# Binary convolution and gated state-space block on one core: order of small steps between two long stages

## The chip, the cores and the metric

The kernel runs on one core of a Trainium2 chip. The time is that of one execution on the device in microseconds, the median of the runs shown. The profile is taken by the hardware profiler from one execution.

## The reference, cut to what matters

The input x is 16 x 112 x 112 x 256, float32. Layer 0 is a group norm, the sign of it, a depthwise 3x3 convolution with signed weights and a residual. Layer 1 takes a group norm of that and

```python
ca_gate = sigmoid(fc(avg) + fc(mx))            # per image and channel
xc = x * ca_gate
m = mean(xc, channels)                          # one value a pixel
y = _s6(m, A, d_w, d_b, B_w, B_b, C_w, C_b)     # scan over the 12544 pixels, 16 states
s = conv7x7([mean(xc), max(xc)], lsa_w)         # per pixel
x2 = xc * sigmoid(y) + xc * sigmoid(s)
out = (x2 - mean(x2)) * rsqrt(var(x2) + EPS) * bn_gamma + bn_beta   # over batch and pixels
return x + relu(out)
```

The scan is h = a * h + b per state, with a = exp(delta * A), and y = sum(h * c). The mean and variance of x2 run over all images, so every x2 is needed once for the statistics and again for the output.

## The kernel before, in words

There are three blocks (`nc.Block`), each with one program an engine. The first makes layer 0 and the channel gates image by image and stores its result x1 in DRAM (`x1_scratch`). It ends with the scans of the first group of 8 images.

The second block is the one the change touches. It has two stages.

*Scans of the second group.* The pixels of the 8 images come in 14 chunks of 896, numbered n = 14 to 27 (NCG = 14, NC = 28). SP loads for each chunk two sets of rows (`load_rows`, L539) and a broadcast row set of 448 KB (`load_spread`, L548) into rings of four places. ACT turns the latter into decays (`make_decay`, L612), PE makes the input of the scan with `spread` (four matmuls, L631), DVE scans (`scan`, L604), PE sums the states with `read_out` (eight matmuls, L640), ACT evacuates y (`evac_y`, L619), and SP stores it to `y_scratch` (L556). In PE's loop the order is: spread of chunk n + 1, at most one *product* (two matmuls, L648), read-out of chunk n. A product is one of 14 steps of the 7x7 convolution over a half of the second group's images. 14 of the first half and 10 of the second stand ahead of the first spread, the other four in chunks 14 to 17. SP's order in chunk n is: load_rows and load_spread of chunk n + 4, store of y of chunk n - 1.

y comes back from DRAM in another layout (`load_y`, L438), in two parts: rows 0 to 63 and rows 64 to 111 of the images, each in two halves q = 0 and q = 1. SP loads q = 0 and POOL q = 1. `load_y` waits until the chunks that it needs are stored. On part 0, DVE joins y (`join_y`, L1746 and L1747) behind scan 25, ACT makes the sigmoids (L1702, L1686), and DVE splits the gate into three bf16 parts (`split_gate`, L1755 to L1760) behind scan 27.

The gates of the last image, which is resident, are stored to `gate_scratch` row by row (`store_last`, L415: four stores for each of three split parts q) and loaded back as 12 rows a strip (`load_gate`, L1562). In part 0 SP, ACT and POOL store one q each, in part 1 SP stores two and POOL one. `store_gates` (L424, 12 stores on POOL) does the same for the other images.

*Statistics.* An image has 7 strips (NS = 7), and xt has one place a strip (`slots`). For each of 112 strips PE broadcasts the gate (L1574, four matmuls), DVE makes u in two operations (L1787, one for each half of the channels), ACT squares it (L1717). SP loads the next image's strip into the place as soon as DVE is done with it (`load_slot`, L1568, 1792 KB, and its gate). In the first strip's turn DVE joins part 1, and in the second's it splits part 1. SP starts with place 0 when all gates of the last image are loaded. After the last strip DVE reduces the sums and makes scale and shift (L1808 to L1833), and makes the first strip of the next pass (`first_strip`, L1799, one for each half j).

The third block, the last pass, makes u again (L2008), applies relu on ACT (L1979), adds x1 on DVE (L2026), transposes on PE (L1958), evacuates on ACT (L1991) and stores (L1928), while SP loads the strips again (L1916).

Of the kernel before, what the change touches and what calls it, by code (L numbers as in the profile page):

```python
# [5 lines left out]
def binary_conv_then_gated_ssm_block(  # L6
# [30 lines left out]
    ACT = mybir.ActivationFunctionType  # L37
# [46 lines left out]
    with ctx:  # L84
# [1526 lines left out]
        bn_ln = sem("bn_ln")  # L1611
        bn_exp = sem("bn_exp")
        gate_ps3 = [banks(psum[:, b * 2048:(b + 1) * 2048], BW) for b in range(2)]

        U3, Q3 = 3, 4

        with nc.Block() as block:
            @block.sync
            def _(sp):
# [14 lines left out]
                for n in range(NCG, NC):  # L1634
                    if n + NROW1 < NC:
                        load_rows(sp, n + NROW1)
                    if n + ND1 < NC:
                        load_spread(sp, n + ND1)
                    if n > NCG:
                        store_y(sp, n - 1)  # L1640
                    if n == NCG + NA:
                        load_y(sp, 1, 0, 0)
                store_y(sp, NC - 1)
                load_y(sp, 1, 0, 1)
                for part in range(2):
                    sp.wait_ge(split_made, 2 + part)
                    store_last(sp, part, 0)
                    if part:
                        store_last(sp, part, 1)
                    sp.wait_ge(last_out[0], 32 * BR * (part + 1))  # L1650
                    sp.wait_ge(last_out[1], 16 * BR * (part + 1))
                    for s in strips_of(part):
                        sp.sem_inc(arrived3[s], 16)
                        load_gate(sp, arrived3, 0, s)
                sp.wait_ge(gates_out, 48 * BR)

                def step(it, more):
                    for n in range(NN):
                        if n < NS or more:
                            sp.wait_ge(u_made3, it * (2 * NN) + 2 * (n + 1) + U3)  # L1660
                            load_slot(sp, arrived3, it * 2 + n // NS, it * 2 + n // NS + 1, n % NS)

                step(0, True)
                sp.wait_ge(gates_out, 96 * BR)
# [5 lines left out]
            @block.gpsimd  # L1670
            def _(pool):
                load_y(pool, 0, 1)
                load_y(pool, 1, 1, 0)
                store_gates(pool, 0, 0, GI)
                pool.wait_ge(split_made, 2)
                store_last(pool, 0, 2)
                load_y(pool, 1, 1, 1)
                pool.wait_ge(split_made, 3)
                store_last(pool, 1, 2)
                store_gates(pool, 1, 0, GI - 1)  # L1680

            @block.scalar
            def _(act):
# [10 lines left out]
                for n in range(NCG, NC):  # L1694
                    if n + 2 < NC:
                        make_decay(act, n + 2)
                    if n > NCG:
                        evac_y(act, n - 1)
                    if n == NC - 3:
                        act.wait_ge(s_made, 4)  # L1700
                        for b in range(2):
                            ins = nc.scalar.activation(s_out[1][:, b * IB * W:(b + 1) * IB * W], s_ps[b], ACT.Sigmoid)  # L1702
                        ins.then_inc(s_sig, 1)
                        sigmoid_y(1, *part_rows(0))
                evac_y(act, NC - 1)
# [6 lines left out]
                def squares3(it):  # L1712
                    for n in range(NN):
                        for j in range(NJ):
                            act.wait_ge(u_made3, it * (2 * NN) + 2 * n + j + 1 + U3)
                            u = xc[n % 2][:, j, :]
                            nc.scalar.activation(u, u, ACT.Square,  # L1717
                                                 accum_out=g2_p[:, n, j, bass.ds(it, 1)]).then_inc(squared3, 1)
# [6 lines left out]
                act.wait_ge(bn_ln, 1)  # L1725
                nc.scalar.activation(bn[:, 5, :], bn[:, 4, :], ACT.Exp, scale=-0.5).then_inc(bn_exp, 1)

            @block.vector
            def _(dve):
# [34 lines left out]
                for n in range(NCG, NC):  # L1764
                    scan(dve, n)
                    if n == NC - 3:
                        join_y(1, 1, *part_rows(0))
                    if n == NC - 1:
                        split_gate(1, 1, *part_rows(0))
# [67 lines left out]
            def _(pe):  # L1837
# [8 lines left out]
                pe.wait_ge(conv_late, 32)  # L1846
                spatial_products(1, 0, 10)
                spread(pe, NCG)
                for n in range(NCG, NC):
                    if n + 1 < NC:  # L1850
                        spread(pe, n + 1)
                    k = 10 + n - NCG
                    spatial_products(1, min(k, 2 * KS), min(k + 1, 2 * KS))
# [19 lines left out]
        u_made4 = sem("u_made4")  # L1873
        relu_made = sem("relu_made")
        x2_made = sem("x2_made")
# [28 lines left out]
        with nc.Block() as block:  # L1904
# [62 lines left out]
            def _(act):  # L1967
# [4 lines left out]

                def relu(it, m):

                    h = m // NS % 2
                    for j in range(NJ):
                        act.wait_ge(u_made4, count(it, m, NJ) + j + 1)
# [3 lines left out]

                relu(0, 0)

# [83 lines left out]
```

## Time and profile before

| | us |
|---|---|
| median of 3 runs | 3281.78 (3280.92 to 3282.52) |
| the profiled execution | 3279.52 |
| its span in the profile | 3277.8 |
| DVE busy | 2972.6 |
| ACT busy | 2703.5 |
| PE busy | 2541.6 |
| POOL busy | 53.2 |

The span is what the profile shows from the first to the last instruction; the profiled execution took 1.7 us more. Busy times are sums over the span. The granted clock of TensorE was 0.849 of full speed on average. All times of rows are from the start of the span.

### The profile page before, as it was taken

The numbers are of one execution on the slowest core, as the hardware profiler recorded it, in microseconds if no ns is written. First come the engines' busy times: TensorE is split into PE (matmuls) and PEld (weight loads), VectorE is DVE, ScalarE is ACT, GpSimd is POOL, SyncE is SP. The second block draws the span as 40 slices with busy tenths as digits, with TensorE's granted clock in tenths as the row PEclk, the third lists the DMA queues.
The fourth block names the chain that finished last, engine by engine and source line by source line (L and its number), as shares of the span: only waits on it lengthen the run. The fifth ranks groups of instructions, "written<-read, shape, count | busy, mean of one in ns | idle before, by whom it ended". The sixth has DMA issues, their size and how long they took to land. (4 is left out here: it accounts for less than half of the span.)

```text
span 3277.8 us, 50171 instructions
## 1 busy us (share of the span) xinstructions
PE 2541.6 (78%) x17105; PEld 1636.8 (50%) x17105; DVE 2972.6 (91%) x4057; ACT 2703.5 (82%) x3772; POOL 53.2 (2%) x103
## 2 busy tenths in 40 slices
PE   7899999999999999999988333333567667666766
PEld 5566666666666666666542000000456555555555
DVE  8789999899998999899987999999999999999997
ACT  6788888888888888888774788888799888888887
POOL 3000000000000000000001100000000000000000
PEclk9999999999999999999997555555688877778777
DMA  8899999999999999999866699999699999999998
GB/s 312 322 373 408 375 369 372 371 406 378 371 371 370 408 377 374 370 373 394 280 187 169 273 421 422 420 420 417 241 429 428 429 429 429 429 429 429 429 429 361
DMA packets 199099, 1228.50 MB, mean 375 GB/s; under 512 B 29793, under 2 KB 38937, under 8 KB 157645
## 3 DMA queue, kind: packets, MB, share of 16 engines
q1 hardware_dynamic: 196012, 1223.42, 92.6%
q0 software_dynamic: 2720, 1.97, 0.3%
q8 instruction: 139, 2.28, 0.3%
q14 instruction: 100, 0.81, 0.1%
q10 hardware_dynamic: 128, 0.01, 0.0%
HBM read 805.14 MB, written 420.17 MB: 374 GB/s over the span
## 5 line engine op out<-in xcount | busy, mean ns | idle before, releaser
L1455 PE MATMUL psum<-signs,taps 128*128 128x448 f16 x4032 | 858.9, 356 | 39.4 <-DVE signs L1084 30.3
L1574 PE MATMUL psum<-signs,picked 12*128 12x448 bf16 x896 | 315.7, 493 | 339.3 <-DMA signs<-gate_scratch 278.9
L1455 PEld LDWEIGHTS psum<-signs,taps 128*128 128x128 f16 x4032 | 385.7, 98 | 367.2 <-DVE signs L1084 49.0
L2008 DVE SCALAR_TENSOR_TENSOR xc<-xt,curs,psum 128x1792 f32<-128x1792 f32 x222 | 452.1, 2078 | 56.4 <-PE psum L1574 44.0
L847 ACT ACTIVATE xt<-psum 128x896 f32<-128x896 f32 x416 | 378.3, 911 | 141.6 <-PE psum L1353 126.0
L1787 DVE SCALAR_TENSOR_TENSOR xc<-xt,curs,psum 128x1792 f32<-128x1792 f32 x224 | 455.9, 2078 | 32.1 <-PE psum L1574 30.6
L1717 ACT ACTIVATE xc<-xc 128x1792 f32<-128x1792 f32 x224 | 380.1, 1697 | 94.1 <-DVE xc L1787 94.0
L1135 DVE CUSTOM_DVE_ANT_0 xt<-work,xt 128x896 f32<-128x896 int8 x416 | 436.0, 1085 | 14.3 <-ACT work L855 14.3
L1353 PE MATMUL psum<-ident,stage 128*128 128x128 f32 x3066 | 409.6, 276 | 20.9 <-POOL over_c L805 6.4
L1979 ACT ACTIVATE xc<-xc,bn,curs 128x1792 f32<-128x1792 f32 x224 | 411.7, 1903 | 13.3 <-issue 4.5
L863 ACT ACTIVATE work<-xt,mean 128x1792 bf16<-128x1792 f32 x208 | 370.3, 1780 | 35.6 <-DVE x1max_p L1135 35.6
L1353 PEld LDWEIGHTS psum<-ident,stage 128*128 128x128 f32 x3066 | 353.5, 142 | 68.6 <-issue 22.0
L1958 PE MATMUL psum<-ident,last_unit 128*128 128x128 f32 x1568 | 277.8, 350 | 140.7 <-DVE last_unit L2026 66.9
L1958 PE MATMUL psum<-ident,signs 128*128 128x128 f32 x1568 | 269.4, 341 | 133.6 <-DVE signs L2026 57.7
L1991 ACT ACTIVATE stage<-psum 128x512 f32<-128x512 f32 x525 | 275.3, 611 | 95.1 <-DMA out_dram<-stage 68.0
L1574 PEld LDWEIGHTS psum<-signs,picked 12*128 12x128 bf16 x896 | 84.4, 114 | 535.3 <-DVE xc L1787 378.1
L1958 PEld LDWEIGHTS psum<-ident,last_unit 128*128 128x128 f32 x1568 | 253.0, 213 | 179.7 <-ACT stage L1991 66.5
L1958 PEld LDWEIGHTS psum<-ident,signs 128*128 128x128 f32 x1568 | 244.1, 211 | 171.4 <-ACT stage L1991 70.5
L1222 DVE TENSOR_TENSOR stage<-xc 128x896 f32<-128x896 f32 x224 | 243.8, 1088 | 61.2 <-ACT xc L894 54.1
L1232 DVE TENSOR_REDUCE pmax<-psum 128x4 f32<-128x512 f32 x448 | 257.6, 617 | 38.7 <-PE psum L1402 36.0
L1084 DVE SCALAR_TENSOR_TENSOR signs<-xt,mean,signs 128x896 f16<-128x896 f32 x208 | 240.3, 1155 | 7.4
L855 ACT ACTIVATE work<-psum,border 128x896 int32<-128x896 f32 x224 | 224.2, 1001 | 18.7 <-PE psum L1455 18.6
(221 smaller groups left out, 2951.9 us busy)
## 6 DMA issues: line engine op xcount, KB each, us to landing
xt<-x_scratch SPq DMA_DIRECT2D x210, 1792.0 KB, 25.3
stage<-x_dram SPq DMA_DIRECT2D x219, 896.0 KB, 9.9
xc<-x_scratch SPq DMA_DIRECT2D x210, 896.0 KB, 9.3
x_scratch<-xt SPq DMA_DIRECT2D x208, 896.0 KB, 9.2
out_dram<-stage SPq DMA_DIRECT2D x75, 1792.0 KB, 21.9
out_dram<-work SPq DMA_DIRECT2D x37, 1792.0 KB, 21.9
x_scratch<-last_unit SPq DMA_DIRECT2D x16, 896.0 KB, 9.9
signs<-ssm_scratch SPq DMA_DIRECT2D x14, 448.0 KB, 4.7
```

What stands on the lines that cost most here:

```text
L847: nc.scalar.activation(dst, src, ACT.Identity, scale=XL if part else 1.0, accum_out=xsum_p[:, j, 2 * u + part:2 * u + part + 1]).then_inc( ...
L863: nc.scalar.activation(squares.rearrange("p (a n) -> p a n", a=2), unit(i, j, u), ACT.Square, scale=-1.0, bias=mean0[:, i % 2, j:j + 1], a ...
L1135: nc.vector.tensor_tensor_reduce(out=px, in0=conv, in1=px, scale=1.0 / XL if part else 1.0, scalar=-3.0e38, op0=ALU.add, op1=ALU.max, accu ...
L1353: ins = nc.tensor.transpose(ring[:, t * P:(t + 1) * P], xin[b][:, t, j * P:(j + 1) * P], ident[:, :])
L1455: return nc.tensor.matmul(turn[h % 2][:, b * 512:b * 512 + HB], taps[:, j, t, :], signs[:, j, r:r + RT // 2, dw:dw + W], start=t == 0, sto ...
L1574: last = nc.tensor.matmul(dst[:, b, :], picked[:, b * P:(b + 1) * P], gate_rows[:, s * BW:(s + 1) * BW], start=True, stop=True)
L1717: nc.scalar.activation(u, u, ACT.Square, accum_out=g2_p[:, n, j, bass.ds(it, 1)]).then_inc(squared3, 1)
L1787: nc.vector.scalar_tensor_tensor(quarters(xc[n % 2][:, j, :]), slot_quarters(s, j), curs[:, h, j:j + 1], gate_quarters(gate_ps3[n % 2]), A ...
L1958: last = nc.tensor.transpose(out_ps[k % 4][:, v * C + j * P:v * C + (j + 1) * P], block_in, ident[:, :])
L1979: nc.scalar.activation(u, u, ACT.Relu, bias=bn[:, 7, j:j + 1], scale=curs[:, h, NJ + j:NJ + j + 1]).then_inc(relu_made, 1)
L1991: nc.scalar.activation(outs[m % NO][:, 2 * k:2 * k + 2, :].rearrange("p t c -> p (t c)"), out_ps[k % 4], ACT.Identity).then_inc(staged, 1)
L2008: nc.vector.scalar_tensor_tensor(quarters(xc[m % 2][:, j, :]), slot_quarters(s, j), curs[:, h, j:j + 1], gate_quarters(gate_ps4), ALU.add, ...
```

## The change

- On PE, four products of the second half stand ahead of the first spread instead of ten, and one product follows in each of the chunks 14 to 23.
- The load of y for part 0, q = 0, is issued by ACT in chunk 24, behind the evacuation of chunk 23, and no longer by SP in chunk 22. DVE's join of part 0 comes behind scan 26 instead of 25, and ACT's sigmoid of it in chunk 26 instead of 25 (the sigmoids of the convolution stay in chunk 25).
- POOL issues the load of y for part 1 ahead of its wait for the first split.
- SP loads place 0 for the next image before it waits for the split of part 1; the other places follow as before. Four of the eight stores of part 1 are issued by ACT, between its squares of the first and the second strip.
- The relu of the first half of the last pass's first strip is made at the end of the second block.

```diff
--- before.py
+++ after.py
@@ -1610,6 +1610,7 @@
         bn_var = sem("bn_var")
         bn_ln = sem("bn_ln")
         bn_exp = sem("bn_exp")
+        relu_made = sem("relu_made")
         gate_ps3 = [banks(psum[:, b * 2048:(b + 1) * 2048], BW) for b in range(2)]
 
         U3, Q3 = 3, 4
@@ -1638,29 +1639,27 @@
                         load_spread(sp, n + ND1)
                     if n > NCG:
                         store_y(sp, n - 1)
-                    if n == NCG + NA:
-                        load_y(sp, 1, 0, 0)
                 store_y(sp, NC - 1)
                 load_y(sp, 1, 0, 1)
+                def step(it, more, first=0):
+                    for n in range(first, NN):
+                        if n < NS or more:
+                            sp.wait_ge(u_made3, it * (2 * NN) + 2 * (n + 1) + U3)
+                            load_slot(sp, arrived3, it * 2 + n // NS, it * 2 + n // NS + 1, n % NS)
+
                 for part in range(2):
+                    if part:
+                        sp.wait_ge(gates_out, 48 * BR)
+                        sp.wait_ge(u_made3, 2 + U3)
+                        load_slot(sp, arrived3, 0, 1, 0)
                     sp.wait_ge(split_made, 2 + part)
                     store_last(sp, part, 0)
-                    if part:
-                        store_last(sp, part, 1)
                     sp.wait_ge(last_out[0], 32 * BR * (part + 1))
                     sp.wait_ge(last_out[1], 16 * BR * (part + 1))
                     for s in strips_of(part):
                         sp.sem_inc(arrived3[s], 16)
                         load_gate(sp, arrived3, 0, s)
-                sp.wait_ge(gates_out, 48 * BR)
-
-                def step(it, more):
-                    for n in range(NN):
-                        if n < NS or more:
-                            sp.wait_ge(u_made3, it * (2 * NN) + 2 * (n + 1) + U3)
-                            load_slot(sp, arrived3, it * 2 + n // NS, it * 2 + n // NS + 1, n % NS)
-
-                step(0, True)
+                step(0, True, 1)
                 sp.wait_ge(gates_out, 96 * BR)
                 if NIT > 2:
                     with sp.Fori(1, NIT - 1) as it:
@@ -1672,9 +1671,9 @@
                 load_y(pool, 0, 1)
                 load_y(pool, 1, 1, 0)
                 store_gates(pool, 0, 0, GI)
+                load_y(pool, 1, 1, 1)
                 pool.wait_ge(split_made, 2)
                 store_last(pool, 0, 2)
-                load_y(pool, 1, 1, 1)
                 pool.wait_ge(split_made, 3)
                 store_last(pool, 1, 2)
                 store_gates(pool, 1, 0, GI - 1)
@@ -1696,11 +1695,14 @@
                         make_decay(act, n + 2)
                     if n > NCG:
                         evac_y(act, n - 1)
+                    if n == NCG + NA + 2:
+                        load_y(act, 1, 0, 0)
                     if n == NC - 3:
                         act.wait_ge(s_made, 4)
                         for b in range(2):
                             ins = nc.scalar.activation(s_out[1][:, b * IB * W:(b + 1) * IB * W], s_ps[b], ACT.Sigmoid)
                         ins.then_inc(s_sig, 1)
+                    if n == NC - 2:
                         sigmoid_y(1, *part_rows(0))
                 evac_y(act, NC - 1)
                 act.wait_ge(split_made, 2)
@@ -1711,6 +1713,9 @@
 
                 def squares3(it):
                     for n in range(NN):
+                        if isinstance(it, int) and n == 1:
+                            act.wait_ge(split_made, 3)
+                            store_last(act, 1, 1)
                         for j in range(NJ):
                             act.wait_ge(u_made3, it * (2 * NN) + 2 * n + j + 1 + U3)
                             u = xc[n % 2][:, j, :]
@@ -1724,6 +1729,10 @@
                 nc.scalar.activation(bn[:, 4, :], bn[:, 3, :], ACT.Ln).then_inc(bn_ln, 1)
                 act.wait_ge(bn_ln, 1)
                 nc.scalar.activation(bn[:, 5, :], bn[:, 4, :], ACT.Exp, scale=-0.5).then_inc(bn_exp, 1)
+                act.wait_ge(first_u, 1)
+                act.wait_ge(cur_made4, 1)
+                nc.scalar.activation(xc[0][:, 0, :], xc[0][:, 0, :], ACT.Relu, bias=bn[:, 7, 0:1],
+                                     scale=curs[:, 0, NJ:NJ + 1]).then_inc(relu_made, 1)
 
             @block.vector
             def _(dve):
@@ -1763,7 +1772,7 @@
                 split_gate(0, 0, 0, H)
                 for n in range(NCG, NC):
                     scan(dve, n)
-                    if n == NC - 3:
+                    if n == NC - 2:
                         join_y(1, 1, *part_rows(0))
                     if n == NC - 1:
                         split_gate(1, 1, *part_rows(0))
@@ -1844,12 +1853,12 @@
                 pe.wait_ge(conv_in, 64)
                 spatial_products(0, 0, 2 * KS)
                 pe.wait_ge(conv_late, 32)
-                spatial_products(1, 0, 10)
+                spatial_products(1, 0, 4)
                 spread(pe, NCG)
                 for n in range(NCG, NC):
                     if n + 1 < NC:
                         spread(pe, n + 1)
-                    k = 10 + n - NCG
+                    k = 4 + n - NCG
                     spatial_products(1, min(k, 2 * KS), min(k + 1, 2 * KS))
                     read_out(pe, n)
                 pe.wait_ge(y_evac, NC)
@@ -1871,7 +1880,6 @@
         gates4, G4 = arrived3, 32 * NB
         spread4 = sem("spread4")
         u_made4 = sem("u_made4")
-        relu_made = sem("relu_made")
         x2_made = sem("x2_made")
         turned4 = sem("turned4")
         staged = sem("staged")
@@ -1970,16 +1978,16 @@
                 for b in range(NO):
                     act.sem_inc(written[b], W4)
 
-                def relu(it, m):
+                def relu(it, m, j0=0):
 
                     h = m // NS % 2
-                    for j in range(NJ):
+                    for j in range(j0, NJ):
                         act.wait_ge(u_made4, count(it, m, NJ) + j + 1)
                         u = xc[m % 2][:, j, :]
                         nc.scalar.activation(u, u, ACT.Relu, bias=bn[:, 7, j:j + 1],
                                              scale=curs[:, h, NJ + j:NJ + j + 1]).then_inc(relu_made, 1)
 
-                relu(0, 0)
+                relu(0, 0, 1)
 
                 def step(it, m0, n):
                     for m in range(m0, m0 + n):
```

## Rows read from the trace of the kernel before

**Rows 1.** The page's slices: busy share of the DMA engines, in tenths
```profile
DMA  8899999999999999999866699999699999999998
```

**Rows 2.** Stages: stretch, length, busy PE PEld DVE ACT POOL (instructions), clock, DMA share, GB/s
```profile
1813.00:1823.00 10.00, 3.50 (x9) 0.86 (x7) 9.52 (x12) 5.81 (x6) 0.00 (x0) 0.50 0.00 0
...
1847.00:2308.00 461.00, 175.04 (x420) 43.80 (x420) 429.21 (x434) 375.40 (x419) 0.00 (x0) 0.50 0.98 408
...
2358.00:3270.00 912.00, 635.91 (x3445) 511.29 (x3444) 849.73 (x443) 770.86 (x970) 0.00 (x0) 0.80 1.00 424
```

**Rows 3.** Timeline of PE and its weight loads in the scans: start, length, what, idle before
```profile
1736.08 20.79 PE L648 MATMUL psum<-stage 112*112 112x448 f32 x48 [2.86 <-PEq L655]
...
1737.68 0.31 PEld L648 LDWEIGHTS psum<-stage 112*112 112x112 f32 x1 [0.44 <-issue]
...
1757.63 0.32 PEld L631 LDWEIGHTS psum<-xc,signs 16*128 16x128 f32 x4 [0.53 <-DMA xc<-ssm_scratch]
...
1765.94 1.12 PE L631 MATMUL psum<-xc,signs 16*128 16x512 f32 x4
...
1767.00 1.00 PE L648 MATMUL psum<-stage 112*112 112x448 f32 x2
...
1767.93 0.58 PE L640 MATMUL psum<-signs 128*32 128x224 f32 x8
...
1773.75 2.07 PE L631 MATMUL psum<-xc,signs 16*128 16x512 f32 x4
...
1775.75 0.98 PE L640 MATMUL psum<-signs 128*32 128x224 f32 x8
...
1776.65 2.07 PE L631 MATMUL psum<-xc,signs 16*128 16x512 f32 x4
```

**Rows 4.** The same table, of short stretches of the scans
```profile
1766.00:1771.00 5.00, 5.00 (x33) 1.43 (x30) 4.56 (x3) 2.57 (x4) 0.00 (x0) 1.00 0.77 176
...
1771.00:1772.00 1.00, 0.13 (x1) 0.00 (x0) 0.76 (x1) 0.58 (x1) 0.00 (x0) 0.88 0.82 208
...
1774.00:1782.00 8.00, 8.00 (x36) 1.86 (x36) 4.99 (x4) 4.59 (x7) 0.00 (x0) 0.50 1.04 244
```

**Rows 5.** Timeline of ACT and DVE in the scans
```profile
1759.53 1.04 ACT L612 ACTIVATE xc<-xc,scol 128x896 f32<-128x896 f32 x1 [2.82 <-DMA xc<-ssm_scratch]
...
1793.26 1.08 DVE L1746 TENSOR_TENSOR stage<-stage 64x896 f32<-64x896 f32 x1 [3.62 <-DMA stage<-y_scratch]
...
1795.77 4.29 DVE L604 TENSOR_TENSOR_SCAN signs<-xc,signs,psum 128x896 f32<-128x896 f32 x2 [0.31 <-DVE stage L1747]
```

**Rows 6.** Waits of SP's queue, 1756 to 1812: total, times, longest
```profile
SPq L435 <- DMA y_scratch<-last_unit: 5.2, 2, 3.9
```

**Rows 7.** Timeline behind the scans: DVE and the queues of SP and ACT
```profile
1805.26 2.77 ACTq L415 DMA_DIRECT2D gate_scratch<-work  x4
...
1810.01 1.59 SPq L1562 DMA_DIRECT2D signs<-gate_scratch  x4
...
1810.92 1.09 DVE L1746 TENSOR_TENSOR stage<-stage 48x896 f32<-48x896 f32 x1 [5.61 <-DMA stage<-y_scratch]
...
1813.38 2.08 DVE L1787 SCALAR_TENSOR_TENSOR xc<-xt,curs,psum 128x1792 f32<-128x1792 f32 x1 [0.25 <-PE psum L1574]
...
1822.84 6.28 SPq L415 DMA_DIRECT2D gate_scratch<-work  x8
...
1832.11 0.36 SPq L1568 DMA_DIRECT2D xt<-x_scratch  x1
```

**Rows 8.** Table by stage, two stretches of the statistics
```profile
1823.00:1832.00 9.00, 1.67 (x4) 0.42 (x4) 9.00 (x9) 6.40 (x7) 8.74 (x15) 0.50 0.21 48
...
1908.00:2300.00 392.00, 146.83 (x353) 36.72 (x352) 361.21 (x366) 315.09 (x354) 0.00 (x0) 0.50 1.00 415
```

**Rows 9.** Timeline at the start of the last pass
```profile
2317.41 3.65 ACT L1979 ACTIVATE xc<-xc,bn,curs 128x1792 f32<-128x1792 f32 x2 [4.23 <-DVEq L2015]
...
2319.32 3.96 DVE L2026 TENSOR_TENSOR last_unit<-xc,xt 128x1792 f32<-128x1792 f32 x2 [2.56 <-ACT xc L1979]
```

## The prediction

> **What bounds the kernel now.** The page's DMA slices come first [rows 1]: 9 tenths nearly everywhere, with a hole of a few slices at 6 in the middle. The table by stage looks into it [rows 2]: DMA stands at 0.00 from 1813 to 1823 us, while the statistics (1847 to 2308) run at 0.98 and the last pass (2358 to 3270) at 1.00. Both long stages are bound by DMA; the hole is a chain of scans, gates and waits. So a microsecond in the hole is one at the end, and so is an earlier start of either stream of transfers. The change touches the hole and both starts.
>
> **Terms.** The sum is made against the profiled execution, 3279.5 us (1.7 us of it outside its span); the median is 3281.8, 2.3 above. A measurement tells about 0.2% (6.6 us) from no change. T is the end of the last scan, 1800.06 (two scans, 4.29 us from 1795.77) [rows 5]. A granted clock of 1.00 is 2.4 GHz, 0.50 is 1.2.
>
> **1. Products (PE).** Six of the ten products that stood ahead of the first scan move into the scans: chunks 14 to 23 have one each, instead of 14 to 17. A product is two matmuls. The front block's 48 take 20.79 us [rows 3], so 12 take at most 5.2 (less, as the slow ones come first): the block ends at about 1752 instead of 1756.9. The first scan may start a microsecond earlier, but the second waits for its decay, and that for a transfer until 1759.53 [rows 5]: the lead is lost, 0.
>
> The cost hangs on the clock. At 2.4 GHz the steps of a chunk start at 1765.94 (spread), 1767.00 (product) and 1767.93 (read-out, 0.58): 1.06 + 0.93 + some 0.6, about 2.6 us. At 1.2 GHz without a product they start at 1773.75, 1775.75 and 1776.65: 2.00 + 0.90 = 2.9 [rows 3]. A product at 1.2 GHz takes 1.5 at least (two matmuls, weight load 0.31 and gap 0.44 each, the row at 1737.68) and 1.9 at most (twice 0.93). I take 1.7, between them, as the two other steps stretch by a little under two. So 4.4 to 4.8 us a chunk, 4.6 taken, against 2.1 for DVE's scan: PE would set the pace.
>
> Which clock? Rows of the stage table show it [rows 4]: 1.00 until 1771; in the next microsecond it falls, with the last product over at 1768.0 and PE busy with spreads and read-outs until then; and from 1774 to 1782 it stays at 0.50 although PE is busy 8.00 of 8.00 us. Spreads and read-outs alone neither hold nor raise it. After the change the last dense product ends at 1752 and the next one follows the second spread, whose rows were awaited until 1757.63 [rows 3]: it starts at 1758 to 1759.6, over 6 us without a product, where 3.8 us cost the clock at 1771.8. So I expect it down as the scans begin. From there a product is 1.7 of 4.6 us, in work that raises nothing. Between "down while the products last" and "up at once" I take the first: 1774 to 1782 is the nearest row.
>
> Worked out: second spread 1757.6, product 1759.6, read-out 1761.3, third spread 1762.2, third scan 1764.3; nine more at 4.6 put chunk 25's scan at 1805.7; the next, with no product before it, at 1808.6, over at 1810.7; the join now behind it 2.25 (two operations of 1.08 [rows 5] and their gaps); last scan 2.15: T = 1815.1, later by **15 us** (13 at 4.4, 17 at 4.8).
>
> The Trainium skill (TensorE: Matmul & The Clock Gate, Part 1) puts it otherwise: there the gate is released by how busy PE has lately been, whatever it runs. By that rule the clock would be back soon, as in the second rival. This trace disagrees for spreads and read-outs (busy 8.00 of 8.00, clock 0.50).
>
> **2. Load of y on ACT, join one scan later.** Before, SP stood 3.9 us ahead of this load [rows 6], and the last chunk's loads queued behind it; DVE stood 3.62 us for y until 1793.26, with two scans still to come [rows 5]. After, SP runs on; ACT issues two loads of about 0.7 us each (four took 2.77 [rows 7]), and only its later evacuations queue behind. With the slow PE of part 1 all of this is hidden: 0. With the full clock it pays: y at about 1793 as before, but only one scan behind the join: T = 1793.3 + 2.25 + 2.15 = 1797.7, a gain of 2.4 (1 to 4, as y may land later or earlier). Sigmoid and its table load move beside the last scan: 0.
>
> **3. POOL's last y load ahead of its gate stores.** DVE stood 5.61 us for y until 1810.92. That load now leaves some 4 us earlier, but DVE's first statistics operation (1813.38) waits for PE's gate, and that for the gate loads of 1810.01, behind the stores of 1805.26 [rows 7]. The gate chain is late next: 0 (0.25 at most, DVE's wait there).
>
> **4. First place ahead of the last gates, four stores from SP to ACT.** Before, the stream starts at 1832.11: DVE's split is over at 1822.84, SP spends 6.28 us on eight stores, waits for them, then loads three gates [rows 7]. After, place 0 is loaded when DVE's first strip is done, two operations of 2.08 behind 1813.38, in the stretch with DMA at 0.00. Later strips come every 4.44 us (353 matmuls, 4 a strip, in 392 us), while DVE needs 4.09 (361.21 busy) [rows 8]; so DMA binds, its start sets the end though DVE has places in hand, and one load less is **4.4 us**. With four stores on each queue the gate loads come 4.75 us behind the split, as in the first part (1805.26 to 1810.01), and the stream 1.2 later (three gate loads, where four took 1.59): 1828.8, **3.3 us** earlier. POOL's stores (share 0.21 from 1823 to 1832 [rows 8]) overlap it 3.3 us longer: 0.7 at most, 0.5 taken. ACT's four issues delay its next square by 0.7, within its two buffers: 0. Together 7.2. Bounds 5 to 8: the early load lands at about 1824, so the stores of 1822.8 can be a microsecond behind it.
>
> **5. First relu inside the statistics' block.** DVE's first addition (2319.32) waits for it; it starts at 2317.41, when the block is over [rows 9]. After, it runs beside DVE's last operation of the block and the addition starts at about 2317.5. Both streams of the last pass hang on it: **1.8 us** (0 if a transfer were late anyway, 2 at most).
>
> Sum: + 15 - 0 - 7.2 - 1.8 = **+ 6 us**: 3285.7 against the profile, **3288.0** against the median. Its own range: 3285 to 3292.
>
> **The rivals.**
> - *The clock stays up.* For it: a product a chunk went with 1.00 until 1768. Against: 6 us without one. Then - 2.4 - 7.2 - 1.8 = - 11.4: 3270.4. Chance 0.22.
> - *It comes back part of the way.* Four slow chunks (chunk 19's scan at 1778.1), then six at 2.6, one at 2.3, scan, join and scan 6.5: T = 1802.5, + 2.5; sum - 6.5: 3275.3. For it: PE is busier than between 1774 and 1782. Chance 0.20, half of it beyond 0.2%.
> - *Slower: the last gates' stores queue behind the early load.* Its 1792 KB lie in the same rings as SP's four small stores; if these wait for all of it, the stream restarts up to 4.4 us late. It decides from 0.6 us of delay on, as the forecast is that near the bound: up to + 10.4, 3292.4. Against: 5.3 us lie between the two issues and DMA is empty. Chance 0.10.
> - *The forecast* holds 0.48, 0.20 of it beyond + 0.2% (a product of 1.8 us or more).
>
> **The numbers.** Faster: 0.22, half of 0.20, and 0.02 for slips: 0.34. Slower: 0.10 and 0.20: 0.30. Same: 0.36. As the cases have both signs, the range runs from the first rival to the third: 3268 to 3292.
>
> **What would show it.** Part 1: granted clock 0.50 from 1758 on, scans 4.4 to 4.8 us apart, DVE waiting for the spread (L631); wrong if they are 2.3 to 2.7 apart at 1.00. Part 2: no stand of SP ahead of the last chunk's loads. Part 3: the join done 3 us before the gate. Part 4: one place load 17.5 us behind T, the stream 28.7 behind T instead of 32.05, and the statistics' end 7 us closer to T. Part 5: the addition in the block's first half microsecond.

## The result, and the profile after

| | before | after |
|---|---|---|
| median | 3281.2 us | 3286.3 us |
| executions | 22, from 3274.5 to 3285.8 | 22, from 3283.7 to 3291.2 |
| ratio | | 1.0019, 95% interval 1.0012 to 1.0025 |
| the profiled execution | 3279.5 us | 3288.2 us |

The forecast was 3288.0, a little over the old time and inside its bound of 0.2%; measured is + 5.1 us between the medians, and the ratio's interval stands for 3.9 to 8.2 us. Two of the twelve executions of experiment 9 below, at 3426.2 and 11148.8 us, were slow ones: its median is that of all twelve (3276.2 without the two), its ratio leaves them out.

The page's slices of the changed kernel, in tenths, the granted clock of TensorE and the DMA engines' share (for the latter [rows 1] has those of before):

```profile
PEclk9999999999999999999996555555678777787787
DMA  8899999999999999999866699999699999999998
```

The hole has the same width on this scale. The clock has six slices at 5 as before; the slice ahead of them, in which it falls, shows 6 where it was 7. The table by stage has the scans in it (columns as in [rows 2]), the second row being the stretch for which [rows 4] has the kernel before:

```profile
1758.00:1803.00 45.00, 45.00 (x138) 11.05 (x136) 21.76 (x11) 14.76 (x21) 4.14 (x7) 0.50 0.71 161
...
1774.00:1782.00 8.00, 8.00 (x28) 2.06 (x28) 2.82 (x3) 2.57 (x4) 0.00 (x0) 0.50 0.47 109
```

PE is busy for all 45 of 45 us at 0.50, while DMA's share is 0.71, and 0.47 in the stretch where it was 1.04. In that stretch the bound has changed, from DMA and PE together to PE alone. PE's timeline shows how (start, length, what, idle before):

```profile
1735.50 16.28 PE L648 MATMUL psum<-stage 112*112 112x448 f32 x36 [2.86 <-PEq L655]
...
1752.33 1.12 PE L631 MATMUL psum<-xc,signs 16*128 16x512 f32 x4 [0.54 <-DMA xc<-ssm_scratch]
...
1756.45 2.07 PE L631 MATMUL psum<-xc,signs 16*128 16x512 f32 x4 [3.01 <-DMA xc<-ssm_scratch]
...
1758.46 1.83 PE L648 MATMUL psum<-stage 112*112 112x448 f32 x2
...
1760.22 0.98 PE L640 MATMUL psum<-signs 128*32 128x224 f32 x8
...
1761.13 2.07 PE L631 MATMUL psum<-xc,signs 16*128 16x512 f32 x4
...
1763.13 1.84 PE L648 MATMUL psum<-stage 112*112 112x448 f32 x2
```

The front block is over at 1751.8 (36 matmuls, 48 before [rows 3]), the first spread comes at once, and then PE stands 3.01 us for the second chunk's rows. The spread took 1.12 us before that wait and 2.07 behind it: the clock fell in the gap, at 1754.15 by the granted clock, 0.7 us after PE had begun to wait. From there spread, product and read-out start at 1756.45, 1758.46, 1760.22 and again at 1761.13 and 1763.13: 2.00 + 1.76 + 0.91 = 4.67 us a chunk. DVE's end of the scans:

```profile
1805.34 2.08 DVE L604 TENSOR_TENSOR_SCAN signs<-xc,signs,psum 128x896 f32<-128x896 f32 x1 [2.59 <-PE psum L631]
...
1808.24 2.08 DVE L604 TENSOR_TENSOR_SCAN signs<-xc,signs,psum 128x896 f32<-128x896 f32 x1 [0.83 <-PE psum L631]
...
1810.24 1.06 DVE L1755 TENSOR_TENSOR stage<-stage 64x896 f32<-64x896 f32 x1
...
1813.08 2.08 DVE L604 TENSOR_TENSOR_SCAN signs<-xc,signs,psum 128x896 f32<-128x896 f32 x1 [0.67 <-DVE stage L1756]
```

From the third on the scans wait for PE: 1.84 us the third, then 2.59 where there is a product before it and 0.83 where there is none. The last scan follows the join. The join of y needs no wait any more, and the last scan is over at 1815.16 (T), 15.1 us later than before. Behind it, DVE and the queues of SP and ACT (to be held against [rows 7]):

```profile
1820.36 2.47 SPq L415 DMA_DIRECT2D gate_scratch<-work  x4
...
1822.95 1.09 DVE L1755 TENSOR_TENSOR stage<-stage 48x896 f32<-48x896 f32 x1 [2.51 <-DMA stage<-y_scratch]
...
1825.43 1.59 SPq L1562 DMA_DIRECT2D signs<-gate_scratch  x4
...
1828.92 2.08 DVE L1796 SCALAR_TENSOR_TENSOR xc<-xt,curs,psum 128x1792 f32<-128x1792 f32 x1 [3.75 <-PE psum L1574]
...
1833.09 0.36 SPq L1568 DMA_DIRECT2D xt<-x_scratch  x1
...
1838.38 3.21 SPq L415 DMA_DIRECT2D gate_scratch<-work  x4
...
1838.38 3.97 ACTq L415 DMA_DIRECT2D gate_scratch<-work  x4
...
1843.86 1.15 SPq L1562 DMA_DIRECT2D signs<-gate_scratch  x3
...
1845.06 0.36 SPq L1568 DMA_DIRECT2D xt<-x_scratch  x1
```

The join of part 1 is done at T + 10.0 instead of T + 13.1, and DVE then stands 3.75 us for PE's gate: the first statistics operation comes at T + 13.8, half a microsecond later than before. The early load of place 0 leaves at T + 17.9, the stream restarts at T + 29.9 (32.05 before). And the start of the last pass (against [rows 9]):

```profile
2319.10 1.08 DVE L1817 TENSOR_REDUCE bnsum<-work 128x16 f32<-128x112 f32 x4
...
2323.57 1.88 ACT L1734 ACTIVATE xc<-xc,bn,curs 128x1792 f32<-128x1792 f32 x1 [1.71 <-DVE curs L1842]
...
2326.09 1.88 ACT L1987 ACTIVATE xc<-xc,bn,curs 128x1792 f32<-128x1792 f32 x1 [0.64 <-DVEq L2023]
...
2326.47 3.96 DVE L2034 TENSOR_TENSOR last_unit<-xc,xt 128x1792 f32<-128x1792 f32 x2 [1.02 <-ACTq L1977]
```

The relu runs beside DVE's last operation of the block, and the first addition comes 7.37 us behind the first reduction instead of 8.91.

### The profile page after: what moved, and what is told of

It reads as the page before. It is cut to its first block and busy times, and to the rows that moved or that the text cites. A ratio compares the mean times of both kernels' runs of the same rounds, so it can differ in the third digit from the quotient of the medians.

```text
span 3286.4 us, 50172 instructions
## 1 busy us (share of the span) xinstructions
PE 2553.5 (78%) x17105; PEld 1636.1 (50%) x17105; DVE 2970.4 (90%) x4057; ACT 2702.5 (82%) x3772; POOL 53.6 (2%) x103
## 5 line engine op out<-in xcount | busy, mean ns | idle before, releaser
L2016 DVE SCALAR_TENSOR_TENSOR xc<-xt,curs,psum 128x1792 f32<-128x1792 f32 x222 | 452.1, 2078 | 58.7 <-PE psum L1574 47.1
L1966 PE MATMUL psum<-ident,signs 128*128 128x128 f32 x1568 | 274.9, 346 | 138.7 <-DVE signs L2034 60.2
L1966 PE MATMUL psum<-ident,last_unit 128*128 128x128 f32 x1568 | 269.1, 341 | 140.4 <-DVE last_unit L2034 59.6
L1966 PEld LDWEIGHTS psum<-ident,last_unit 128*128 128x128 f32 x1568 | 243.8, 211 | 178.5 <-ACT stage L1999 72.4
```

What stands on the lines that cost most here:

```text
L1966: last = nc.tensor.transpose(out_ps[k % 4][:, v * C + j * P:v * C + (j + 1) * P], block_in, ident[:, :])
L2016: nc.vector.scalar_tensor_tensor(quarters(xc[m % 2][:, j, :]), slot_quarters(s, j), curs[:, h, j:j + 1], gate_quarters(gate_ps4), ALU.add, ...
```

## The experiments

All times of this table but the medians are distances within the profiled execution, from DVE's first operation of the second block to T, from T to the first reduction behind the statistics, from there to the first addition of the last pass, and from that to the end. The ratio is one of mean times, to executions of the kernel before that were taken beside each experiment. Their medians were 3280.3 us for experiments 1 to 4, 3279.6 for 5 to 8 and 3280.3 for 9 to 11, and differences to before in the text are from these.

| kernel | median | ratio to before (95%) | block to T | T to reduction | to addition | to end |
|---|---|---|---|---|---|---|
| before | 3281.2 | | 60.2 | 510.4 | 8.9 | 958.5 |
| after | 3286.3 | 1.0019 (1.0012 to 1.0025) | 75.6 | 503.9 | 7.4 | 959.9 |
| 1 ten ahead | 3269.3 | 0.9970 (0.9959 to 0.9981) | 58.9 | 503.7 | 7.4 | 957.8 |
| 2 four ahead only | 3293.9 | 1.0043 (1.0030 to 1.0056) | 74.0 | 510.1 | 8.9 | 958.7 |
| 3 gap filled | 3270.3 | 0.9974 (0.9962 to 0.9987) | 58.4 | 503.5 | 7.4 | 958.1 |
| 4 place and stores only | 3272.9 | 0.9974 (0.9965 to 0.9983) | 57.9 | 504.2 | 8.9 | 960.2 |
| 5 two products a chunk | 3274.7 | 0.9986 (0.9977 to 0.9995) | 63.6 | 504.1 | 7.4 | 958.3 |
| 6 relu only | 3278.0 | 0.9992 (0.9984 to 1.0001) | 58.8 | 510.9 | 7.4 | 959.0 |
| 7 y only | 3277.2 | 0.9992 (0.9983 to 1.0001) | 57.4 | 510.5 | 8.9 | 958.2 |
| 8 split first | 3268.0 | 0.9962 (0.9950 to 0.9975) | 58.7 | 501.4 | 7.4 | 958.4 |
| 9 place only | 3276.5 | 0.9983 (0.9974 to 0.9992) | 64.1 | 506.5 | 8.9 | 960.2 |
| 10 split and place | 3268.9 | 0.9964 (0.9951 to 0.9976) | 58.5 | 500.5 | 7.4 | 958.0 |
| 11 join last | 3266.9 | 0.9963 (0.9950 to 0.9976) | 57.4 | 502.9 | 7.4 | 957.7 |

The table shows which stage each part touches: the products and y the first column of distances, place and stores the second, the relu the third. The last pass takes 957.7 to 960.2 us whatever was changed, which is what the profiles scatter by there.

### 1. Ten products ahead again, all else as changed

```diff
-                spatial_products(1, 0, 4)
+                spatial_products(1, 0, 10)
...
-                    k = 4 + n - NCG
+                    k = 10 + n - NCG
```

> The changed kernel with ten products ahead of the first scan again and one in chunks 14 to 17. Theory (the products in the scans cost through the half clock): the clock stays at 1.00 until about 1771, chunk 26's scan is over near 1790, y lands near 1793, the last scan ends at 1797.7 instead of 1815.2, and the gains of the other parts stand: 17.5 us less than the changed kernel, about 3269, 12 us under the kernel before. Rival (another part of the change costs, such as y's load on ACT or the early place): no better than the kernel before, 3281 or more.

Measured: 3269.3 us. Granted clock of two stretches of the scans:

```profile
1758.00:1770.00 12.00, 10.91 (x60) 3.24 (x60) 10.05 (x5) 5.94 (x8) 0.00 (x0) 1.00 0.83 195
...
1774.00:1782.00 8.00, 7.91 (x32) 1.95 (x28) 5.06 (x3) 3.85 (x6) 0.00 (x0) 0.50 0.95 241
```

And DVE at their end:

```profile
1790.96 2.08 DVE L604 TENSOR_TENSOR_SCAN signs<-xc,signs,psum 128x896 f32<-128x896 f32 x1 [0.82 <-PE psum L631]
...
1794.20 1.08 DVE L1755 TENSOR_TENSOR stage<-stage 64x896 f32<-64x896 f32 x1 [1.16 <-DMA stage<-y_scratch]
...
1797.07 2.08 DVE L604 TENSOR_TENSOR_SCAN signs<-xc,signs,psum 128x896 f32<-128x896 f32 x1 [0.67 <-DVE stage L1756]
```

The clock is full until 1772, a product a chunk or not, and half behind it. Chunk 26's scan is over at 1793.0 (expected near 1790), y lands at 1794.2 (1793) and T is 1799.15 (1797.7). So undoing part 1 alone takes 17 us off (3286.3 to 3269.3), and what is left of the change is worth 11 us. The theory stands, the rival falls. The 17 us go over two series of executions, in which the kernel before differs by about 1 us.

### 2. The moved products alone

The kernel before with the two lines above changed the other way.

> The kernel before with the products moved alone. Theory: scans 4.67 us apart at a granted clock of 0.50 from chunk 16 to 25, join hidden but two scans behind it, last scan over at about 1814 instead of 1800.1: 14 us more than before, 3295. Rival (DVE or DMA sets the pace and PE's part is hidden): scans 2.9 apart at most, 3281.

Measured: 3293.9 us. DVE's last scans:

```profile
1805.80 2.08 DVE L604 TENSOR_TENSOR_SCAN signs<-xc,signs,psum 128x896 f32<-128x896 f32 x1 [2.59 <-PE psum L631]
...
1810.29 4.29 DVE L604 TENSOR_TENSOR_SCAN signs<-xc,signs,psum 128x896 f32<-128x896 f32 x2 [0.31 <-DVE stage L1747]
```

The scan of chunk 25 starts 4.67 us behind chunk 24's, and T is 1814.6, as expected. DVE and DMA do not hide PE. The clock fell at 1755.70 here, again while PE stood for the second chunk's rows (2.33 us).

### 3. The gap filled

```diff
+                def fill(m):
+                    for _ in range(m):
+                        nc.tensor.matmul(bank[3][0:H, 224:448], bands[:, 0, 0, :], fpad[0][:, GI:GI + 2, 0:W],
+                                         start=True, stop=True)
...
                 spread(pe, NCG)
+                fill(8)
                 for n in range(NCG, NC):
```

> The changed kernel, with eight half-size products whose results are not used between the first and the second spread, where PE stood 3 us for rows. Theory (it is the gap that costs the clock, and one product a chunk then holds it): clock 1.00 on into the scans, scans 2.6 us apart while they have products, the last one over at about 1798, about 3269. Rival (products in the scans cost their time whatever the clock, or the clock falls anyway with one product a chunk): scans 4.67 apart, 3286.

The results of these matmuls are read by nobody; they only keep PE at work. Measured: 3270.3 us. PE from the first spread on, and a stretch of the scans:

```profile
1754.85 1.12 PE L631 MATMUL psum<-xc,signs 16*128 16x512 f32 x4 [0.46 <-DMA xc<-ssm_scratch]
...
1755.90 3.28 PE L1855 MATMUL psum<-stage 112*112 112x224 f32 x16
...
1760.40 1.12 PE L631 MATMUL psum<-xc,signs 16*128 16x512 f32 x4 [1.22 <-DMA xc<-ssm_scratch]
...
1761.45 1.01 PE L648 MATMUL psum<-stage 112*112 112x448 f32 x2
...
1762.38 0.59 PE L640 MATMUL psum<-signs 128*32 128x224 f32 x8
```

```profile
1770.00:1790.00 20.00, 19.27 (x113) 5.58 (x110) 16.73 (x9) 9.95 (x17) 0.00 (x0) 1.00 0.95 237
```

The filler (line 1855) takes 3.28 us of the gap, the next spread still takes 1.12, and the clock stays at 1.00 until 1791, when the last product has been over for 4.4 us. PE's order in the scans is that of the changed kernel, with the same ten products, and PE does more work in all; only the clock differs. So the moved products cost nothing where the clock is held: the gap costs the clock, and the clock costs the time. The filler's matmuls have the shape of a product's, 224 columns wide instead of 448, so this does not tell PE's idle time from time without such matmuls. Most scans now wait for ACT's decays, and these for their transfers, 2.3 to 2.8 us apart. This is not faster than ten ahead, as y's landing (1795.5) again decides when the last scan can start.

The twelve executions of this kernel fall into two groups: nine took 3266.2 to 3272.2 us, the profiled one among them, and three 3281.5 to 3283.4, with a mean granted clock of 0.850 to 0.854 in the nine and 0.848 or 0.849 in the three. The clock may have fallen in those three in spite of the filler; no trace shows it.

### 4. Place and stores alone

```diff
                 for part in range(2):
+                    if part:
+                        sp.wait_ge(gates_out, 48 * BR)
+                        sp.wait_ge(u_made3, 2 + U3)
+                        load_slot(sp, arrived3, 0, 1, 0)
                     sp.wait_ge(split_made, 2 + part)
                     store_last(sp, part, 0)
-                    if part:
-                        store_last(sp, part, 1)
...
-                step(0, True)
+                step(0, True, 1)
...
+                        if isinstance(it, int) and n == 1:
+                            act.wait_ge(split_made, 3)
+                            store_last(act, 1, 1)
```

> The kernel before with the first place loaded ahead and four of the last stores on ACT, nothing else. Theory: one load of 4.4 us less in the stream and its restart 2.2 earlier, as in the changed kernel: 6.5 us less than before, 3275. Rival (the statistics give it back to DVE, or the stores queue behind the load): within 1 us of before, 3281.

Measured: 3272.9 us, 7.4 less than before, with 6.1 of it between T and the reduction. The two starts of the stream (T = 1798.3):

```profile
1816.11 0.36 SPq L1568 DMA_DIRECT2D xt<-x_scratch  x1
...
1828.06 0.36 SPq L1568 DMA_DIRECT2D xt<-x_scratch  x1
```

Nothing is given back to DVE: the theory stands.

### 5. Two products a chunk

```diff
-                spatial_products(1, 0, 4)
...
-                    k = 4 + n - NCG
-                    spatial_products(1, min(k, 2 * KS), min(k + 1, 2 * KS))
+                    k = 2 * (n - NCG)
+                    spatial_products(1, min(k, 2 * KS), min(k + 2, 2 * KS))
```

> The changed kernel with none of the second half's products ahead of the first spread and two in each of chunks 14 to 20: more of PE's work in the scans, and the gap as it is. Theory (the clock stays down in the changed kernel because one product in 4.67 us is too little of it, so two raise it): 1.00 again by the third chunk, then scans 3.4 us apart, last scan over at about 1804, 11 us under the changed kernel, 3275. Rival (the clock does not come back among scans, whatever runs): scans 6.4 apart, last one over at about 1822, 3293.

Measured: 3274.7 us. PE's first spread, PE across the change of the clock, and two stretches around it:

```profile
1753.94 2.04 PE L631 MATMUL psum<-xc,signs 16*128 16x512 f32 x4 [4.25 <-issue]
...
1765.60 3.33 PE L648 MATMUL psum<-stage 112*112 112x448 f32 x4
...
1768.86 0.61 PE L640 MATMUL psum<-signs 128*32 128x224 f32 x8
...
1769.39 1.12 PE L631 MATMUL psum<-xc,signs 16*128 16x512 f32 x4
...
1770.45 1.76 PE L648 MATMUL psum<-stage 112*112 112x448 f32 x4
```

```profile
1760.00:1768.00 8.00, 8.00 (x20) 2.40 (x18) 4.34 (x3) 4.21 (x5) 0.00 (x0) 0.50 1.05 220
...
1769.00:1788.00 19.00, 19.00 (x104) 6.18 (x101) 11.47 (x6) 8.14 (x13) 0.00 (x0) 1.00 0.73 173
```

With no product of the second half ahead, PE now stands 4.25 us before the first spread, and the clock falls there, at 1751.89. It is back at 1768.95, as the second pair of products ends. The four matmuls of a pair take 3.33 us ahead of that and 1.76 behind it, and chunks come 3.26 apart instead of 6.17. All 14 products of the second half are now in the scans, four more than in the changed kernel, and the median is 11.6 us lower. So the half clock of the changed kernel is not a lasting state of this stage: one product in 4.67 us did not bring the clock back in ten chunks, two in 6.17 did by the end of the second.

### 6. The relu alone

```diff
+                act.wait_ge(first_u, 1)
+                act.wait_ge(cur_made4, 1)
+                nc.scalar.activation(xc[0][:, 0, :], xc[0][:, 0, :], ACT.Relu, bias=bn[:, 7, 0:1],
+                                     scale=curs[:, 0, NJ:NJ + 1]).then_inc(relu_made, 1)
...
-                relu(0, 0)
+                relu(0, 0, 1)
```

> The kernel before with the first relu in the statistics' block alone. Theory: DVE's first addition 7.4 us behind the first reduction instead of 8.9, and the end 1.5 us earlier: 3279.3. Rival (the last pass gives it back): the addition earlier by as much, the end the same, 3280.8.

Measured: 3278.0 us beside 3279.6, ratio 0.9992 (0.9984 to 1.0001). The addition comes 7.4 us behind the reduction, in every kernel that has this part, and 8.9 in every one that has not. That the 1.5 us reach the end is likely by the median and not settled by the interval.

### 7. y's load, join and sigmoid alone

```diff
-                    if n == NCG + NA:
-                        load_y(sp, 1, 0, 0)
...
+                    if n == NCG + NA + 2:
+                        load_y(act, 1, 0, 0)
...
-                    if n == NC - 3:
+                    if n == NC - 2:
                         join_y(1, 1, *part_rows(0))
```

> The kernel before with y's first part loaded by ACT, DVE's join behind scan 26 and ACT's sigmoid a chunk later. Forecast's term: SP's stand ahead of the last loads is gone, y lands near 1793 as before, one scan less behind the join, last scan over 2.4 us earlier: 3278.5. Rival (y's load leaves ACT later by what SP's stand had cost, so that the join comes as much later as it is followed by less): the end within 1 us of before.

Measured: 3277.2 us beside 3279.6, ratio 0.9992 (0.9983 to 1.0001). In its profile the join follows scan 26 at once, where DVE stood 3.62 us for y before, and 1.96 and 2.19 in experiments 4 and 6. What this is worth is less clear. T comes 57.4 us behind the block's start. Three kernels whose scans are those of before have 60.2, 57.9 and 58.8 there (before, 4 and 6), and three with ten ahead and this part 58.9, 58.7 and 58.5 (1, 8 and 10). The means differ by less than the profiles scatter: a gain of up to 2.4 us is neither shown nor ruled out.

### 8. A version built on this: the last gates split first

With y's second part there at T + 8 to 10 and DVE standing over 3 us for PE's gate, DVE can split the last gates ahead of its first strip. Ten products ahead, then:

```diff
                         if isinstance(it, int) and n == 0:
                             join_y(2, 1, *part_rows(1))
-                        if isinstance(it, int) and n == 1:
                             split_gate(2, 1, *part_rows(1))
```

The early load goes, ACT's four stores move ahead of its first square, and the stores of the two parts count on semaphores of their own.

> Ten products ahead, the other parts of the change, but the last gates split ahead of DVE's first strip (it stands 3.3 us there), so that all places are loaded from then on and no early load is needed. Expected: split over 15.5 us behind the last scan instead of 23, its gates loaded at 21, stream from there instead of one load at 17.9 and the rest from 29.8; first strip 2 us later. One stream start at 21 against one worth 25.4: 4.4 us under the kernel with ten ahead, 3265. Rival (the later first strip or the stores in the stream's way give it back): 3269.

Measured: 3268.0 us. SP's queue (T = 1801.42):

```profile
1817.97 3.20 SPq L415 DMA_DIRECT2D gate_scratch<-work  x4
...
1823.44 1.15 SPq L1562 DMA_DIRECT2D signs<-gate_scratch  x3
...
1824.69 0.36 SPq L1568 DMA_DIRECT2D xt<-x_scratch  x1
```

The split is over at T + 16.6 (expected 15.5), the stream starts at T + 23.3 (21), and the reduction comes 2.3 us nearer to T than in experiment 1 instead of 4.4. y landed at T + 7.9, and from SP's first store to the first load of the gates 5.5 us passed.

### 9. The early load alone

Experiment 4 with all eight stores on SP as before.

> The kernel before with the first place loaded ahead of the last gates, all eight stores on SP as before. Theory (the early load takes one load of 4.4 us out of a stream that binds, the moved stores add 2.2): restart 32 us behind the last scan as before, the first reduction 4.4 us nearer to it, 506 instead of 510.4; about 3275.2. Rival (it is the earlier restart that pays, and the stores behind the early load lose its gain): reduction at 510 behind it, 3279.6.

Measured: 3276.5 us, ratio 0.9983 (0.9974 to 0.9992). The reduction comes 506.5 us behind T: 3.9 less than before, with the restart at T + 32.5. The load taken out of the stream is worth nearly the 4.4 expected, the stores on ACT the other 2.3 of experiment 4.

This profile shows something else. Its scans are those of the kernel before, yet T comes 64.1 us behind the block's start, 4 us later than in the kernel before:

```profile
1758.00:1760.00 2.00, 1.52 (x5) 0.57 (x6) 1.89 (x1) 0.00 (x0) 0.00 (x0) 1.00 1.00 233
...
1761.00:1775.00 14.00, 14.00 (x46) 3.46 (x42) 8.32 (x4) 6.55 (x9) 0.00 (x0) 0.50 0.77 192
```

```profile
1772.66 2.08 DVE L604 TENSOR_TENSOR_SCAN signs<-xc,signs,psum 128x896 f32<-128x896 f32 x1 [2.60 <-PE psum L631]
...
1780.24 2.08 DVE L604 TENSOR_TENSOR_SCAN signs<-xc,signs,psum 128x896 f32<-128x896 f32 x1 [0.83 <-PE psum L631]
```

In this execution the clock fell at 1760.80 and not near 1772. With three chunks still to have a product, scans came 4.67 us apart until the products were over, as in the changed kernel, and 2.91 from 1777.33 to 1780.24 and on. In the eight other profiles with the same order on PE (before, experiments 1, 4, 6, 7, 8, 10 and 11) it fell between 1771.75 and 1773.27.

### 10. Split first, and place 0 loaded while SP waits

```diff
                     store_last(sp, part, 0)
+                    if part:
+                        sp.wait_ge(gates_out, 48 * BR)
+                        sp.wait_ge(u_made3, 2 + U3)
+                        load_slot(sp, arrived3, 0, 1, 0)
...
-                step(0, True)
+                step(0, True, 1)
```

> The kernel with the split first, and its place 0 loaded while SP waits for the last gates' stores (it is free 20.6 us behind the last scan, the stream started at 23.3). Expected: stream from 21, 2.2 us less than with the split first alone: 3266. Rival (the load stands in the way of the stores and of the gates): no gain, 3268.

Measured: 3268.9 us. SP's queue (T = 1799.17):

```profile
1819.75 0.36 SPq L1568 DMA_DIRECT2D xt<-x_scratch  x1
...
1823.70 0.35 SPq L1568 DMA_DIRECT2D xt<-x_scratch  x1
```

Place 0 leaves at T + 20.6 as expected, and the next at T + 24.5. The reduction is 0.9 us nearer to T than in experiment 8, not 2.2: place 1 comes as late as it did there, since SP now issues the last gates behind place 0. The medians do not tell the two apart.

### 11. The join behind the last scan

```diff
-                    if n == NC - 2:
-                        join_y(1, 1, *part_rows(0))
                     if n == NC - 1:
+                        join_y(1, 1, *part_rows(0))
                         split_gate(1, 1, *part_rows(0))
```

ACT's sigmoid moves behind its last evacuation, and y's second part counts on semaphores of its own.

> The same with DVE's join of y's first part behind the last scan instead of behind chunk 26's. Expected: last scan over 3.5 us earlier and the split begun 0.5 us earlier, y's second part out of DRAM 3 us earlier, so that the second split no longer waits for it and ends 12 us behind the first one's end, not 12.6 and more: about 3 us less, 3263. Rival (y's first part lands no earlier, and the sigmoid behind the join now stands open): the same as before this step.

Measured: 3266.9 us, ratio 0.9963 (0.9950 to 0.9976). Block to T is 57.4 and T to the reduction 502.9: 560.3 together, against 559.0 in experiment 10. T comes 1.0 us earlier than there and not 3.5: the scans are 2.91 us apart, and y had kept DVE for 0.65 us only. Y's second part is there in time, as expected, but the join (2.2 us) and the sigmoid (DVE waits 1.14 us for it) now stand open between the last scan and the split, and DVE then waits 1.65 us for the second part's sigmoid, where it was 1.14. Not told apart from experiment 10. Experiments 1, 8, 10 and 11 all beat both kernels; their intervals overlap, and the order among them is open.

## Why the prediction was right, and where a term was off

**Part 1, + 15 us: 15.4.** Each link of it is in the profile: front block over at 1752, the second scan waiting for its decay (it starts at 1759.38), the clock down as the scans begin, PE the bound. The product's slot was 1.76 us (forecast 1.7, 1.5 to 1.9), the chunk 4.67 (4.6, 4.4 to 4.8), T 1815.16 (1815.1). That T fits to 0.1 us is luck in part: the third scan came 1.0 us sooner than forecast (1763.31 for 1764.3), nine chunks at 4.67 took 0.6 more, and 2.76 us passed for the join between the last two scans instead of 2.25. Experiments 1 and 2 give the term by itself as 17 and about 14 us.

The doubtful choice, between a clock that comes back and one that does not, came out as the nearest row had it, with a chance of 0.48 put on it. The reason given for the fall fits less well. It counted over 6 us without a product, as 3.8 had cost the clock before; but the clock fell 2.4 us behind the last product, 0.7 into PE's wait. Experiment 3 shows that what PE does in that stretch made the difference, and not whether it is the idleness or the missing products. The first rival's state is that kernel's: it was put at - 11.4 us, that kernel's median lies 10.0 below that of before, and the median of its nine shorter executions 11.0. Experiment 5 has the clock of the second rival, which took two products a chunk; with one, in the changed kernel, it did not come back.

By the Trainium skill (TensorE: Matmul & The Clock Gate, Part 1) the clock follows how busy PE has been. In the changed kernel PE was busy 45.00 of 45 us at 0.50. With busy time as its measure, the skill's rule is against this trace; what PE ran mattered.

**Part 2, 0 with the slow PE: right.** ACT's evacuation of chunk 23 comes at 1803.30, the load behind it, and DVE joins at once. The - 2.4 at the full clock, a term of the first rival, is the one left open by experiment 7.

**Part 3, 0: right**, by the profile of after alone: the join is done 3 us earlier and DVE waits 3.75 us for PE's gate instead of 0.25. It was not run by itself.

**Part 4, - 7.2: measured 6.4 in the changed kernel, 6.1 by itself.** The early load was sized rightly (4.4 forecast, 3.9 in experiment 9), and the stores did not queue behind it: they were issued 5.3 us later and took SP 3.21 us. What was too high is the restart. It came at T + 29.9 and not at 28.7, since ACT needed 3.97 us for its four stores, not the 2.77 of the first part on which the 4.75 us rested (5.48 measured), and since the first strip came 0.44 us later. The restart was 2.15 us earlier, not 3.3. The slower rival, the stores behind the early load, did not come about: without an early load, in experiment 8, the same stretch took 5.47 us.

**Part 5, - 1.8: 1.54.** The addition started 0.38 us behind the start of the second half's relu, the last block's first operation, where the forecast had it at once.

**The sum.** The recorded addition is 0.2 us high: 3279.5 and 6.0 make 3285.5, and 3287.8 against the median. The terms as measured are + 15.4 from the block's start to T, - 6.4, - 1.5: + 7.5. The profiles differ by 8.6 (1.4 of it in the last pass), the medians by 5.1, so the median's nearness to + 6 says less than the terms do. Executions of one kernel scatter by more than the terms 2, 3 and 5, and experiment 9 shows one way in which they do: by where the clock falls.

## What to carry to other kernels

Before work of a slow engine's is taken out of a dense stretch, look at what stands where it was: here the six products cost nothing in their new place when the gap was filled (the profile of experiment 3), and 17 us with the gap of 3 us that they left. Where a stage is full of small-tile matmuls, keep the granted clock beside the busy time of PE, as a full PE may be a slow one. And where a stream of transfers binds a long stage, its start sets its end, even where the engines that it feeds still have work in hand: one place loaded early, while the DMA engines were idle, gave 4 us (experiment 9).

## What the runs showed of the hardware

- PE at 45.00 of 45 us busy stayed at 0.50 (1.2 GHz) in the changed kernel; with two products a chunk, as busy, it was back at 1.00 as the second pair ended (experiment 5), and with one a chunk it kept 1.00 in the profile in which the gap had been filled (experiment 3).
- In nine profiles with the same order on PE the clock fell at 1760.80 once (experiment 9) and between 1771.75 and 1773.27 in the other eight. From the block's start to T it took 64.1 us with the early fall and 57.4 to 60.2 without. Why it fell early is open.
- Four stores of 2.6 KB took ACT 3.97 us to issue and SP 3.21 at the same time, while four of 3.5 KB had taken 2.76 and 2.47 just before. Experiments 4 and 8 show the same of the smaller ones (4.12 and 3.19, 4.15 and 3.20). Why they take longer was not tried.
